# Shifted-window attention and a Fourier mixing layer: scores and weighted sums over 128 rows with block-diagonal moving operands

## What is computed

```python
qkv = xw @ qkv_w.T + qkv_b                    # windows of 4x4 pixels: N = 16 tokens, 4 heads of 16 channels
attn = einsum('whnd,whmd->whnm', q / |q|, k / |k|) * scale + bias
out = einsum('whnm,whmd->whnd', softmax(attn), v) @ proj_w.T + proj_b
x = x + layernorm(out, norm1_g, norm1_b)
x = x + layernorm(gelu(x @ fc1_w.T + fc1_b) @ fc2_w.T + fc2_b, norm2_g, norm2_b)
y = moving_average(x, 25) + irfft(mix(rfft(x - moving_average(x, 25))[:128]))
```

## Time and profile before

| | |
|---|---|
| median of 3 runs | 8508.97 us (8503.53 to 8515.7) |
| the profiled execution's own time | 8510.45 us |
| its span, first to last instruction | 8508.3 us |
| mean granted PE clock | 0.973 of full |
| busy share of the span: PE, ACT, DVE, POOL | 94%, 72%, 65%, 61% |
| PE matmul records | 293,684 |
| main loop | about 0.2 to 7.3 ms |

### The profile page before, as it was taken

The page is one execution under the profiler, slowest core; times in us unless marked ns, Lnnn a source line. Parts: engine busy times, 40 slices in busy tenths (PEclk is TensorE's granted clock), DMA queues, the critical chain, the costliest instruction groups (busy, mean ns, idle before and its releaser), DMA issues.

```text
span 8508.3 us, 658585 instructions
## 1 busy us (share of the span) xinstructions
PE 8028.3 (94%) x293684; PEld 5317.5 (62%) x293684; DVE 5495.2 (65%) x8029; ACT 6156.0 (72%) x8530; POOL 5157.8 (61%) x5127
## 2 busy tenths in 40 slices
PE   8899999999999999999999999999999999878786
PEld 5556666666666666666666666666666666667675
DVE  1467777777777777777777777777777777322221
ACT  1478888888888888888888888888888888422221
POOL 0367777777777777777777777777777777100000
PEclk9799999999999999999999999999999999989898
DMA  3122222222222222222222222222222222699999
GB/s 99 52 50 59 58 58 59 59 59 58 58 58 57 56 58 59 59 58 58 59 59 58 58 59 59 59 58 58 56 56 58 59 59 58 202 357 331 359 331 336
DMA packets 1187119, 834.40 MB, mean 98 GB/s; under 512 B 633233, under 2 KB 1043217, under 8 KB 1182867
## 3 DMA queue, kind: packets, MB, share of 16 engines
q1 hardware_dynamic: 1182404, 698.61, 31.9%
q10 hardware_dynamic: 4608, 134.22, 3.7%
HBM read 412.97 MB, written 285.21 MB: 82 GB/s over the span
## 4 chain that ended last, share of the span: by engine, by line
PE 73%; SPq 14%; DMA 7%; issue 4%; ACT 1%; DVE 0%; ACTq 0%; POOL 0%; POOLq 0%; DVEq 0%
PE ps L501 12%; PE ps L479 11%; SPq L335 10%; PE ps L581 9%; PE ps L542 9%; PE ps L554 9%; PE ps L462 8%; PE ps L526 5%; PE ps L513 5%; DMA out<-arena 4%; DMA arena<-in_x 3%; PE ps L450 3%; SPq L346 2%; SPq L341 2%; PE ps L424 1%
## 5 line engine op out<-in xcount | busy, mean ns | idle before, releaser
L953 POOL TENSOR_TENSOR arena<-arena 128x512 f32<-128x512 f32 x1024 | 1043.2, 1040 | 886.3 <-PE ps L501 886.3
L479 PEld LDWEIGHTS ps<-arena 32*32 32x32 f32 x131072 | 1236.8, 106 | 511.5 <-issue 503.6
L501 PEld LDWEIGHTS ps<-arena 32*32 32x32 f32 x131072 | 1288.5, 103 | 289.1 <-issue 256.4
L501 PE MATMUL ps<-arena 32*32 32x16 f32 x131072 | 1422.7, 186 | 19.0 <-issue 17.4
L479 PE MATMUL ps<-arena 32*32 32x16 f32 x131072 | 1346.9, 180 | 24.8 <-issue 18.0
L985 POOL TENSOR_TENSOR arena<-arena 128x512 f32<-128x512 f32 x512 | 712.9, 1392 | 950.0 <-DVE arena L844 950.0
L805 DVE TENSOR_TENSOR arena<-ps,arena 128x768 f32<-128x768 f32 x1024 | 980.8, 958 | 358.7 <-PE ps L462 346.8
L462 PEld LDWEIGHTS ps<-arena 64*128 64x128 f32 x8192 | 648.4, 188 | 837.0 <-issue 829.9
L694 ACT ACTIVATE arena<-ps,arena 128x1024 f32<-128x1024 f32 x1024 | 1137.8, 1111 | 6.5
L581 PE MATMUL ps<-xch,amat 128*128 128x256 f32 x4096 | 911.4, 386 | 241.7 <-ACT arena L718 195.0
L542 PE MATMUL ps<-arena 64*128 64x512 f32 x4096 | 1031.5, 621 | 2.8 <-ACT arena L682 2.3
(11 more groups left out here) (89 smaller groups left out, 13925.4 us busy)
## 6 DMA issues: line engine op xcount, KB each, us to landing
arena<-in_x SPq DMA_DIRECT2D x4096, 32.0 KB
arena<-arena SPq DMA_DIRECT2D x1024, 128.0 KB, 2.3
y<-ystripe SPq DMA_DIRECT2D x256, 512.0 KB
amat<-mix SPq DMA_DIRECT2D x512, 256.0 KB, 3.4
xch<-y SPq DMA_DIRECT2D x512, 256.0 KB, 4.1
out<-arena ACTq DMA_DIRECT2D x32, 4096.0 KB, 27.1
mix<-amat SPq DMA_DIRECT2D x64, 256.0 KB, 2.0
wri<-in_w_real SPq DMA_DIRECT2D x64, 64.0 KB, 1.8
```

What stands on the lines that cost most here:

```text
L479: ins = mm(S(sl)[r, c0 + e:c0 + 32:2], qT[r, sl, q, e:64:2], kT[r, sl, q, e:32:2], start=True, stop=True, tile_position=(32 * cg, 32 * cg))
L501: ins = mm(PV[32 * h:32 * h + 32, b, c0:c0 + N], vexp[r, sl, h, :, :], pT[r, sl, h // 2, h % 2, :], start=True, stop=True, tile_position=( ...
L953: tt(vexp.rearrange("p s h e d -> p (s h) e d")[:, :, e, :], qkv[ring(g, 4)][:, 2].rearrange("p s (h d) -> p (s h) d", h=HEADS), par[:, e: ...
```

## The change

Scores and weighted sums contract over all 128 partitions. The moving operand is made block-diagonal: `kTx` and `pTx`, 2,048 columns each, hold zeros (set once) and four diagonal blocks, which SP spreads with four DMAs each from `kT` and `pT` in every group. One product then has 128x32 weights and 64 moving columns, and there are 32 for the scores and 32 for the weighted sums, on the four column tiles (0, 32p). Groups are 4 rows by 256 pixels, so x is loaded with two DMAs of 128 KB. q and k are projected together (8 products with 128 columns) and v apart from a regrouped copy of x (8 products with 64 columns); before there were 8 with 192. The offsets of the norms are folded into the bias of the first layer and into `gain2`, so both POOL additions go; a copy of x for the residual is made by DMA (`copy_x`). The square of q and k moves from ACT to POOL. The logarithms of the two norms share an instruction, and so do the exponentials. PSUM banks are dealt out anew: bank 5 is used in turn by the weighted sums, the turned x and a variance, bank 4 by the scores and the other variance. The lists are rewritten and LAG is 10. The diff, cut to its core:

```diff
...
-LAG = 7
-SWAP = 4
+LAG = 10
...
+        offs = carve(4)
+        o1, o2, g1, g2 = (offs[:, i:i + 1] for i in range(4))
+        be1, be2, o12 = (carve(1) for _ in range(3))
...
+        xT, xTc = [carve(512) for _ in range(2)], carve(512)
+        xr8 = [carve(512) for _ in range(8)]
+        qk = [carve(1024).rearrange("p (w s n) -> p w s n", w=2, s=SLOTS) for _ in range(2)]
+        vb = [carve(512) for _ in range(4)]
...
+        kTx = rows[:, 0:2048].rearrange("p (c s q t) -> p c s q t", c=4, s=SLOTS, q=2)
+        pTx = rows[:, 2048:4096].rearrange("p (c q x h n) -> p c q x h n", c=4, q=2, x=SLOTS, h=2)
...
         MA, MB = ps[:, 0:2, :], ps[:, 2:4, :]
-        PV = ps[:, 4:6, 0:256]
+        SB, PV = ps[:, 4, :], ps[:, 5, :]
...
+        XT = PV
...
             def load_x(s, q, g):
-                need(sp, xT_ps, before(g))
-                for a in range(2):
-                    src = xr[bass.ds(s * ROWS, ROWS)][:, a * HALF + q * QW:a * HALF + q * QW + QW, :]
-                    for p in range(4):
-                        sp.dma_start(xin[:, p, a * C:a * C + C], src[:, p * 8:p * 8 + 8, :]).then_inc(x_in, 16)
+                if there(g):
+                    need(sp, xT_ps, before(g))
+                    for a in range(2):
+                        src = xr[bass.ds(s * ROWS + q * WIN, WIN)][:, a * HALF:(a + 1) * HALF, :]
+                        sp.dma_start(xin[:, :, a * C:a * C + C], src.rearrange("r p c -> p r c")).then_inc(x_in, 16)
+
+            def copy_x(g):
+                if there(g):
+                    need(sp, xT_sb, g)
+                    sp.dma_start(xr8[ring(g, 8)], xT[ring(g, 2)]).then_inc(xr_in, 16)
+
+            def spread_p(g):
+                if there(g):
+                    need(sp, pT_sb, g)
+                    for c in range(4):
+                        r = slice(32 * c, 32 * c + 32)
+                        sp.dma_start(pTb[r, c, :], pT[r, :]).then_inc(pTx_in, 16)
 
...
+            def spread_k(g):
+                if there(g):
+                    need(sp, kT_sb, g)
+                    for c in range(4):
+                        r = slice(32 * c, 32 * c + 32)
+                        sp.dma_start(kTb[r, c, :], kT[r, :]).then_inc(kTx_in, 16)
...
+            def turn(b, k):
+                copy_x(Group(b, k - 1))
+                spread_p(Group(b, k - 5))
+                swap_halves(Group(b, k - 7))
+                spread_k(Group(b, k - 3))
...
+                def project_qk(g):
+                    if there(g):
+                        need(pe, xT_sb, g)
+                        after(pe, (gelu0, i9), (qk_sb, before(g)))
+                        for p in range(4):
+                            for a in range(2):
+                                ins = mm(MA[:, a, p * P:(p + 1) * P], xT[ring(g, 2)][a * C:a * C + C, p * P:(p + 1) * P],
+                                         wqkv[a * C:a * C + C, 0:2 * C], start=True, stop=True, tile_position=(a * C, 0))
+                        ins.then_inc(qk_ps, 1)
+
+                def project_v(g):
+                    if there(g):
+                        need(pe, xTc_sb, g)
+                        after(pe, (gelu1, i9), (vb_sb, before(g)))
+                        for c in range(4):
+                            for a in range(2):
+                                ins = mm(MB[:, a, c * C:(c + 1) * C],
+                                         xTc[a * C:a * C + C, c * P:(c + 1) * P],
+                                         wqkv[a * C:a * C + C, 2 * C:3 * C], start=True, stop=True, tile_position=(a * C, 0))
+                        ins.then_inc(v_ps2, 1)
...
+                def scores(g):
+                    if there(g):
+                        need(pe, qT_sb, g)
+                        need(pe, kTx_in, g, 16 * 4)
+                        if there(i8) or there(i10):
+                            need_norms(pe, l12_sb, i8, i10)
                         else:
...
+                            need(pe, biased, before(g))
+                        settled(pe)
...
+                        sv = SB.rearrange("p (q a c m e) -> p q a c m e", q=2, a=2, c=4, e=2)
+                        for a in range(2):
                             for q in range(2):
                                 for e in range(2):
-                                    c0 = SC(sl) + q * 32
...
+                                    for p in range(4):
+                                        ins = mm(sv[32 * p:32 * p + 32, q, a, :, :, e], qT[:, a * 4 + p, q, e:64:2],
+                                                 kTx[:, :, a * 4 + p, q, e:32:2], start=True, stop=True,
+                                                 tile_position=(0, 32 * p))
+                        ins.then_inc(S_ps, 1)
...
+                def weighted(g):
+                    if there(g):
+                        need(pe, pTx_in, g, 16 * 4)
+                        need(pe, v0_sb, g)
+                        need(pe, v1_sb, g)
+                        if there(i8) or there(i10):
+                            need_norms(pe, l12_sb, i8, i10)
                         else:
+                            need(pe, oT_sb, before(g))
+                            need(pe, xT_sb, i1)
                         settled(pe)
+                        ov = PV.rearrange("p (a s c n) -> p a s c n", a=2, s=4, c=4)
+                        for a in range(2):
+                            for c in range(4):
+                                for h in range(HEADS):
+                                    ins = mm(ov[32 * h:32 * h + 32, a, :, c, :], vexp[:, a * 4 + c, h, :, :],
+                                             pTx[:, :, h // 2, a * 4 + c, h % 2, :], start=True, stop=True,
+                                             tile_position=(0, 32 * h))
+                        ins.then_inc(pv_ps, 1)
...
                         need(pe, sq2_sb, h)
-                        after(pe, (xT_sb, i0), (gelu0, i6), (l1_sb, before(g), before(h)))
+                        need(pe, biased, i4)
+                        after(pe, (xT_sb, i0), (oT_sb, i6))
...
+                            after(pe, (qk_sb, i2), (gelu0, before(g)))
                         else:
-                            after(pe, (qkvB_sb, i0), (qkvA_sb, i0), (gelu1, before(g)))
+                            after(pe, (vb_sb, i2), (gelu1, before(g)))
...
+                first_layer(i9, 0, MA, fc1a_ps)
+                first_layer(i9, 1, MB, fc1b_ps)
+                weighted(i6)
+                scores(i4)
                 turn_x(i0)
-                scores(i2, 1)
-                second_layer(i6, 0, fc2a_ps)
-                second_layer(i6, 1, fc2b_ps)
-                project_qkv(i0, 0, MA, qkvA_ps)
-                weighted(i3, 0, pvA_ps)
-                variances(i4, i6)
-                project_qkv(i0, 1, MA, qkvB_ps)
-                weighted(i3, 1, pvB_ps)
-                first_layer(i5, 0, MB, fc1a_ps)
-                first_layer(i5, 1, MA, fc1b_ps)
-
-            over_groups(pe, step, 1)
+                project(i7)
+                second_layer(i9, 0, fc2a_ps)
+                second_layer(i9, 1, fc2b_ps)
+                project_qk(i1)
+                project_v(i1)
+                variances(i7, i9)
+
+            over_groups(pe, step, 4)
...
                 def keep_x(g):
                     if there(g):
                         need(act, xT_ps, g)
-                        need(act, qkvB_ps, before(g))
-                        need(act, xo_sb, before(g))
-                        f(xT.rearrange("p s (n j e) -> p (s n) j e", j=WIN, e=2),
...
-                def square(g):
-                    if there(g):
-                        need(act, qkvB_sb, g)
-                        need(act, summed, before(g))
-                        f(sq, qkv[ring(g, 4)][:, 0:2].rearrange("p w s n -> p (w s n)"), ACT.Square).then_inc(squared, 1)
...
+                def log_norms(g, h):
+                    if there(g) or there(h):
+                        need_norms(act, var_ps, g, h)
+                        k = slice(0 if there(g) else 1, 2 if there(h) else 1)
+                        f(l12[:, k, :], VV[:, k, :], ACT.Ln, bias=eps).then_inc(l12_sb, 1)
+
+                def root_norms(g, h):
+                    if there(g) or there(h):
+                        need_norms(act, l12_sb, g, h)
                         need(act, dn1_sb, before(g))
...
+                keep_o(i6)
+                gelu(i9, 0, MA, fc1a_ps, fc2a_ps, gelu0)
+                gelu(i9, 1, MB, fc1b_ps, fc2b_ps, gelu1)
+                square1(i7)
+                keep_x(i0)
                 act.preload_act_table_set(EXP_SET)
+                square2(i9)
                 log_norm(i2)
-                square2(i7)
                 root_norm(i2)
-                exponent(i3)
-                log1(i5)
-                log2(i7)
-                root1(i5)
-                root2(i7)
-                keep_o(i4)
+                exponent(i4)
+                log_norms(i7, i9)
+                root_norms(i7, i9)
```

(108 more changed lines are left out.)

246 lines of the change are left out of this document (80 added, 166 removed).

## The result

| | before | changed |
|---|---|---|
| median | 8510.15 us | 8847.16 us (8819.61 to 8871.83, 4 runs) |
| ratio | | 1.0395, 95% interval 1.0364 to 1.0427 |
| step of the main loop | 13.51 us | 2000/140 = 14.29 us |
| mean granted PE clock | 0.973 | 0.905 |

The prediction said 7570 us, and its range ended at 8250. The loop accounts for nearly all of the loss of 337 us: from the first turned x to the last the traces have 7265 us where they had 6956. The two steps of the table were read in the middle of the loop and overstate it (512 x 0.78 = 399 us), since the kernel before had some slower steps at the loop's start.

The account below looks back on a forecast made before the run. PE, 13.3 busy us of a 13.51 us step, was taken as the bound; after the change PE, DVE, SP and the chain lie close. At 11.6 us a step, 1593 + 5939 + 35 = 7567, so 7570 us; range 7100 to 8250.

Parts of the forecast that it names:

- PE's own work: PE's busy time a step: 6.4 kept, 2.4 scores and weighted sums, 2.2 projection, 11.0 us against 13.3.
- rival 2: On PE, weight loads set the pace: 12.3 to 13.2 us a step with waits, 7925 to 8385 us; chance 0.22.
- rival 4: On PE, loads don't overlap products when both cover all rows: PE 24 us a step, 13,900 us; chance 0.04.
- The other sums: Busy time a step on ACT 10.2 us and POOL 10.1; SP's issues 0.72 us each, 9.8 us in all.
- The chain and SP's list: Loop from weighted sums through copy, square, swap and variances, 11.3 to 11.8 us; new waits for spread operands have slack.
- rival 3: SP's queue backs up after stores: thirteen issues at 1.1 us, 14.7 us a step, 9155 us; chance 0.08.
- about a half: The DMAs' busy share in the loop after the change, up from 0.26; argued against SP's queue backing up.
- VectorE: 11.05 us predicted: DVE's busy time a step: 10.6 us from moved and added operations, plus dependent pairs, 11.05.
- five dependent pairs: In DVE's new list, instructions now directly behind ones they depend on: some 0.1 us each, between nothing and 0.2.
- the folded offset, said to cost nothing: In DVE's list, the norms' offsets were to cost nothing: one more operand in an instruction that exists.
- The regrouping copy: DVE's added regrouping of x for v: 0.48 us a step, taken like the gain.
- The clock: PE's granted clock in the loop: under 1.00 the forecast fails; at 0.89 a step would be 12.4 us.

Follow-up runs that it names:

- e1: The changed kernel with SP issuing the next x load before the spreads of k, and the store after both: 8522.43 us, ratio 1.0008.
- e6: e1 with PE's loop unrolled by two in place of four, part of the output not the reference's: 8095.08 us, ratio 0.9507.
- e4: The kernel before with PE's loop unrolled by four and nothing else changed: 11801.09 us, ratio 1.3865.
- e2: The changed kernel with the square of q and k back on ScalarE: 8813.7 us, ratio 1.0351.
- e12: The changed kernel with only the two VectorE edits of e9: 8556.21 us, ratio 1.0054.
- e9: e6 made whole by GpSimd copying x1, plus VectorE's clamp taken out and its gain reading PSUM: 7833.98 us, ratio 0.92.
- e10: e9 with PE's projection ahead of the turning of x: 7809.39 us, ratio 0.9173.

## Why the prediction was wrong, step by step

**PE's own work: right, even too high.** By starts in undisturbed steps the weighted sums take 0.92 to 0.99 us and the scores 1.1 to 1.2 (1.2 each predicted, down from 2.8 and 2.6). q and k take 0.99 us and v 0.94: 1.9 where 2.2 was predicted. Rivals 2 and 4 fall as far as weight loads go: the 64 records of a part go by at 14 to 19 ns each, not 26, and with loads of about 115 ns each they can't be paying them in series. The Trainium skill's sentence that a weight load overlaps products in flight only if its row group differs ("TensorE: Matmul & The Clock Gate", Part 3, Packing small matmuls) isn't borne out by these products. The same section also has a load pulled ahead where it goes into the background weight buffer, and with that sentence the trace agrees.

**The other sums: right.** ScalarE has 1436.65/140 = 10.3 us a step (10.2 predicted), GpSimd 9.9 (10.1). SP's issues of the spreads go by at 0.60 us each in a free row (four in 2.42), less than the 0.72 taken.

**The chain and SP's list: the step that failed first.** The prediction named the order, "then `spread_k`, on which the next scores wait, then the next x", and priced every wait but the last. It gave the new waits slack one by one and never asked when x would land. Before, the eight loads were issued from 4004.94 on for a turn at 4014.69. Now the load stood behind the last spread of the step before, and in one step of four behind a store too: there the two issues were held 1.8 us each and the second landed 3.4 us later than in the earlier trace rows. The earlier trace rows had shown the hold-up, 8.09 us for eight issues behind a store against 0.72 each in a free row. This is rival 3's mechanism (chance 0.08), SP's order with issues held up after a store, but not at its price: thirteen slow issues would have been needed there, where the two of x and their landing sufficed. The argument against that rival was a mean: "about a half" is right for the loop (0.45), but in the 6 us behind a store the DMAs were busy 0.89. e1 shows 325 us for this step.

**PE's loop unrolled by four: costed at nothing, in silence.** The last line of PE's part of the diff was read as bookkeeping for the rings. e6 against e1 gives it 427 us, and e4 shows that unrolling costs time in the kernel before too, with nothing else changed. Whoever costs an edit has to cost the loop that holds it.

**VectorE: 11.05 us predicted, 11.8 measured.** The terms that were mis-sized are the gain and the clamp, 0.54 and 0.59 us over. That is more than the whole miss of 0.75; the 0.45 added for five dependent pairs hides the rest. Both were taken at the lengths that they have while GpSimd waits. The kernel before had them there in every step: the gain's spread of 471 to 484 ns in it was luck of the order. The new list put them beside the expansion of v, whose two instructions take 2.2 us together, and the stripe writer. A small part is the gain's own: the folded offset, said to cost nothing, stands in an instruction that takes 545 to 549 ns beside an idle GpSimd (e2) and not 479, whether by the second operand or by its new place right behind the norm. The regrouping copy was right in the mean, 517 ns for 480, but it has 363 beside an idle GpSimd and up to 1233 beside a busy one. The trace of after shows the clamp ending with the stripe writer: the writer runs from 4014.99 for 1.51 us, the clamp from 4015.29 for 1.26. The two edits together are worth 291 us on the changed kernel (e12) and 408 us where VectorE binds (e9); the clamp's own 0.15 us a step is in both, and no run has one edit without the other.

The Trainium skill states this ("SBUF — State Buffer", Who interferes with whom): VectorE and GpSimd share one pair of SBUF ports, taken for a whole instruction by VectorE's two-port modes (copies and tensor_scalar from SBUF can be in one) or by an operation with two SBUF inputs while GpSimd reads SBUF. The traces agree: the copy and the tensor_scalar from SBUF were held (up to 1233 and 1408 ns) and end at a fixed distance behind GpSimd's instruction, the two-input form was held (1295 ns in the mean), the form from PSUM never (809 to 812 ns).

**The clock** was thought of only under rival 2 and as a sign of failure; every term of the sum stands at 1.00. It added to the other losses: 0.91 in the loop, and 0.97 to 0.98 once the long waits of PE had gone (e6, e9, e10). No experiment held the clock apart from the waits, so its share isn't known.

These prices don't add up, since each fault hides part of the others. With all three mended, and the projection first (e10), a step takes 12.2 us against 11.6 forecast, and 7809 us lies within the range given. That is not a hit: e10 is another kernel, and its step is at the upper end of the forecast's 11.2 to 12.2. It shows that the idea with these mends is worth about 8%, where the forecast had 11%; the kernel as written lost it.

What stays open: how much of e10's 12.2 us is the swap's DMA (129.9 us of PE's waits in 2000) and how much the tie between VectorE and GpSimd.

## What to carry to other kernels

When an engine's work shrinks, walk the queue that feeds it to the end, the transfers without a new wait included: ask of each load when it is issued now, and what stands in front of it. Read the unrolling of a hardware loop as an edit with a price: count the instructions of its body and compare the instruction queue's bytes. When GpSimd is busy beside VectorE, look there at copies and tensor_scalar from SBUF and at operations with two SBUF inputs, the short ones above all; transposes and reductions from SBUF weren't held here, and a PSUM operand may look dearer and be cheaper. And where a transfer stands behind a burst, don't judge its wait by the DMAs' mean share of the whole loop.

## What the runs showed that I hadn't expected

- A PE body of 1129 records (before) or 2 x 392 = 784 (e6) is not loaded again in the loop; code is loaded all through with one of 1574 (11.88 MB in the run), and one of about 4500 costs 39% (41.91 MB). The limit lies between 1129 and 1574; the runs don't place it closer.
- A 64-column operation on VectorE that takes 150 to 156 ns in the kernel before took up to 1271 ns beside GpSimd, eight times its length.
- After a 3.11 us stand of PE, the next 8 records took 3.79 us in place of 1.99.
